# Two chained attention layers on one core: reciprocals and block transpositions by pairs of heads, low parts as steps of their own, and a newly drawn order of all steps

## What is computed

```python
# layer 0
h = jnp.concatenate([x, latents], axis=1)
q = (latents @ q_w + q_b).reshape(b, k_len, NH, DH)
kv = (h @ kv_w + kv_b).reshape(b, p + k_len, NH, DH, 2)
attn = jnp.einsum('bkhd,bnhd->bhkn', q, kmat) / DH
attn = softmax(where(full_mask, attn, -inf))
attn_out = jnp.einsum('bhkn,bnhd->bkhd', attn, v).reshape(b, k_len, H) @ out_w + out_b + residual
out = rmsnorm(attn_out, postnorm_w)
out = gelu(out @ mlp_w1 + mlp_b1) @ mlp_w2 + mlp_b2 + residual
# layer 1, on that result
xn = (input - mu) * rsqrt(var + EPS) * gamma + beta
att = softmax(einsum('nhqc,nhkc->nhqk', q * scale, k * scale))
y = einsum('nhqk,nhkc->nhqc', att, v)
out = input + einsum('co,nos->ncs', Wo, y) + bo
```

## Time and profile before

| | |
|---|---|
| median of 3 runs | 673.29 us (672.45 to 673.97) |
| the profiled execution, its own time | 670.9 us |
| its span, first to last instruction | 669.1 us |
| PE busy | 590.7 us, 88% |
| DVE busy | 575.9 us, 86% |
| ACT busy | 491.9 us, 74% |
| POOL busy | 402.8 us, 60% |
| mean granted TensorE clock | 0.962 |

### The profile page before, as it was taken

The page is one execution under the profiler, slowest core; times in us unless marked ns, Lnnn a source line. Parts: engine busy times, 40 slices in busy tenths (PEclk is TensorE's granted clock), DMA queues, the critical chain, the costliest instruction groups (busy, mean ns, idle before and its releaser), DMA issues.

```text
span 669.1 us, 21092 instructions
## 1 busy us (share of the span) xinstructions
PE 590.7 (88%) x8436; PEld 471.7 (70%) x8436; DVE 575.9 (86%) x1358; ACT 491.9 (74%) x1875; POOL 402.8 (60%) x392
## 2 busy tenths in 40 slices
PE   3597798799899989999899989999899989898985
PEld 3487776687688767776678667877678767676763
DVE  4685689699978999699987999799987999689993
ACT  1655777868787876878777876879778777867781
POOL 0520438477648857577548857578547857467672
PEclk9777997899999999999999999999999999898987
DMA  9700000011111111111111021111101121010110
GB/s 270 149 33 2 32 18 2 17 30 50 29 41 35 28 45 47 27 42 38 29 42 33 25 49 26 50 41 34 26 16 34 26 50 26 17 26 18 31 37 9
DMA packets 49826, 26.46 MB, mean 40 GB/s; under 512 B 37792, under 2 KB 48064, under 8 KB 49728
## 3 DMA queue, kind: packets, MB, share of 16 engines
q1 hardware_dynamic: 49728, 25.11, 14.6%
HBM read 22.99 MB, written 2.10 MB: 38 GB/s over the span
## 4 chain that ended last, share of the span: by engine, by line
PE 44%; DVE 40%; ACT 8%; DMA 3%; issue 2%; POOL 2%; SPq 1%
PE bank L561 42%; DVE nm L998 10%; DVE E1b L1007 8%; DVE nm L862 4%; DVE hm L882 4%; ACT E1b L1135 3%; DVE QS L991 2%; DMA E1b<-in_w 2%; ACT E L1065 2%; PE bank L681 2%; DVE ZS L1013 1%; ACT hm L1104 1%; DVE rs L1003 1%; DVE aos L808 1%; DVE xnb L983 1%
## 5 line engine op out<-in xcount | busy, mean ns | idle before, releaser
L1192 POOL TENSOR_TENSOR E1b<-E1b,rs 128x512 f32<-128x512 f32 x256 | 267.1, 1066 | 104.4 <-DVE rs L1003 100.4
L1135 ACT ACTIVATE E1b<-bank,nm 128x256 f32<-128x256 f32 x512 | 237.6, 499 | 72.9 <-DVE nm L998 72.6
L1007 DVE STREAM_TRANSPOSE E1b<-E1b 128x512 f32<-128x512 f32 x256 | 170.3, 688 | 2.7 <-POOL E1b L1192 1.9
L998 DVE TENSOR_REDUCE nm<-bank 128x2 f32<-128x512 f32 x256 | 165.4, 672 | 5.3 <-PE bank L561 4.7
L561 PE MATMUL bank<-E1b,CT 32*64 32x256 f32 x4096 | 124.2, 390 | 21.7 <-ACT E1b L1135 10.2
L561 PE MATMUL bank<-ctx,QS 64*128 64x256 f32 x1024 | 139.0, 400 | 3.2 <-ACT QS L1125 1.6
L561 PEld LDWEIGHTS bank<-E1b,CT 32*64 32x64 f32 x4096 | 98.3, 136 | 42.6 <-ACT E1b L1135 12.2
L1135 ACT ACTIVATION_READ_ACCUMULATOR E1b<-bank,nm 128x1 f32 x512 | 118.1, 231 | 0.0
L561 PEld LDWEIGHTS bank<-ctx,QS 64*128 64x128 f32 x1024 | 93.6, 190 | 28.6 <-issue 6.9
L1065 ACT ACTIVATE E<-bank,nm 128x128 f32<-128x128 f32 x256 | 90.4, 405 | 19.6 <-DVE nm L862 19.6
L1162 POOL TENSOR_TENSOR E<-E,rs 128x512 f32<-128x512 f32 x56 | 58.9, 1055 | 39.0 <-DVE rs L868 38.8
(11 more groups left out here) (103 smaller groups left out, 785.1 us busy)
## 6 DMA issues: line engine op xcount, KB each, us to landing
CT<-in_hT SPq DMA_DIRECT2D x256, 32.0 KB, 1.8
hraw<-in_hT SPq DMA_DIRECT2D x8, 512.0 KB, 3.2
ctx<-in_ctx SPq DMA_DIRECT2D x16, 256.0 KB, 3.9
xnat<-in_xn SPq DMA_DIRECT2D x8, 256.0 KB, 2.7
E1b<-in_w SPq DMA_DIRECT2D x2, 1024.0 KB, 11.7
out<-y SPq DMA_DIRECT2D x16, 128.0 KB, 1.8
E1b<-in_kvw SPq DMA_DIRECT2D x2, 256.0 KB, 4.4
mski<-in_msk SPq DMA_DIRECT2D x32, 1.0 KB
```

The lines of the kernel that those rows point to most:

```text
L998: e.tensor_reduce(nm1[:, u % 16, :], bank[place["S", u]][:, :].rearrange("p (i t) -> p i t", i=2), AX.X, ALU.max, negate=True).then_inc(dv ...
L1007: e.transpose(E1b[:, u % 16, :, :], E1b[:, u % 16, :, :]).then_inc(dve_steps, 1)
L1135: t = e.activation(E1b[:, r, i, :], bank[bk][:, i * 256:(i + 1) * 256], ACT.Exp, bias=nm1[:, r, i:i + 1], scale=1.0, accum_out=sum1[:, r, ...
L1192: e.tensor_tensor(E1b[:, u % 16, :, :], E1b[:, u % 16, :, :], rs1[:, u % 16, :].unsqueeze(2).to_broadcast([128, 2, 256]), ALU.mult).then_i ...
```

## The change

- `N` and `U` are steps of two units: one reciprocal of 128x4 and one transposition of 128x1024 where there were two of each. `N` waits for both exponentials, `U` for both rescalings.
- `hlo` is a step of its own that GpSimd or DVE may run; the mask row is a new step `mk`. `K`, `Q`, `V` wait for `hlo`, the scores `s` for `mk`. The next load `lh` is issued after both.
- The split of the attention output becomes `xo` (high part, ACT or DVE) and `xol` (low part, GpSimd or DVE).
- `SHIFT` may hold values for group 0 alone (names that end in 0), and the planner counts TensorE's steps 1.6 times in the first 60 us of its time (`COLD`). `SHIFT`, `LATE`, `PREP`, `COST`, `HEADAT` and `STAY` have new numbers, so the whole order is another.

```diff
-NP = ('POOL',)
+COLD = (60000, 1.6)
-PREP = 9
-LATE = (-4, -3, 2, 0, 0.5, 4, 3, 3)
-STAY = 1.5
+PREP = 10
+LATE = (-4, -3, -1, 0.5, -0.5, 4, 3, 4)
+STAY = 1
-HEADAT = -40
+HEADAT = -100
-    "hhi": (760, 840), "hlo": (1750, 1830), "wk": (1030, 1110), ...
+    "hhi": (760, 840), ("hlo", "DVE"): (1550, 1630), ("hlo", "POOL"): (2500, 2550), "mk": (210, 290), ...
...
+                    if e == "PE" and now < COLD[0]:
+                        hold, lasts = int(hold * COLD[1]), int(lasts * COLD[1])
...
-        add("hlo", g, on=A, at=at(), after=[("hhi", g), None if g else ("m0",)] + (
+        add("hlo", g, on=G + A, at=at(), after=[("hhi", g)])
+        add("mk", g, on=A, at=at(), after=[("lh", g) if g else ("m0",)] + (
             [("s", g - 2, c) for c in range(2)] if g >= 2 else []))
...
-        add("xo", g, on=A, at=at(), after=[("o1", g, c) for c in range(2)] + ([("O", g - 1)] if g else []))
+        add("xo", g, on=P + A, at=at(), after=[("o1", g, c) for c in range(2)] + ([("O", g - 1)] if g else []))
+        add("xol", g, on=G + A, at=at(), after=[("xo", g)])
...
-            add("N", u, on=A, at=u + LATE[3], after=[("E", u)])
-            add("Np", u, on=NP, at=u + LATE[4], after=[("N", u)])
-            add("U", u, on=A, at=u + LATE[5], after=[("Np", u)])
+            if h % 2:
+                add("N", u - 1, on=A, at=u + LATE[3], after=[("E", u - 1), ("E", u)])
+                for i in (u - 1, u):
+                    add("Np", i, on=G, at=i + LATE[4], after=[("N", u - 1)])
+                add("U", u - 1, on=A, at=u + LATE[5], after=[("Np", u - 1), ("Np", u)])
...
                     load_h(g)
+                    w.wait_ge(*done("mk", g - 1))
                     load_mask(g)
...
-                    e.reciprocal(rs1[:, u % 16, :], sum1[:, u % 16, :]).then_inc(dve_steps, 1)
+                    e.reciprocal(rs1[:, k:k + 2, :], sum1[:, k:k + 2, :]).then_inc(dve_steps, 1)
...
-                    e.transpose(E1b[:, u % 16, :, :], E1b[:, u % 16, :, :]).then_inc(dve_steps, 1)
+                    e.transpose(E1b[:, k:k + 2, :, :], E1b[:, k:k + 2, :, :]).then_inc(dve_steps, 1)
```

More of the change, by code:

```diff
@@ L48 @@
     "var": (130, 300), "q": (853, 1100), "S": (860, 1050), "Z": (3700, 3900), "Y": (1715, 1950),
[3 rows of a table removed]
[2 rows of a table added]
+    "hhi": (760, 840), ("hlo", "DVE"): (1550, 1630), ("hlo", "POOL"): (2500, 2550), "mk": (210, 290), "wk": (1030, 1110), "wq": (1030, 1110), "wv": (1030, 1110),
     ("Qe", "DVE"): (802, 890), "qs": (400, 500), "smax": (608, 692), "sn": (85, 169),
-    ("snp", "DVE"): (610, 694), "o1": (401, 480), "obtd": (3800, 3880), "w1": (1600, 1680),
[4 rows of a table removed]
+    ("snp", "DVE"): (850, 930), "o1": (401, 480), "obtd": (3800, 3880), "w1": (1600, 1680),
+    "w2": (1050, 1130), "Me": (601, 683), "WSe": (600, 680), "uue": (250, 330), "Mg": (400, 480), ("xo", "DVE"): (450, 530), ("xo", "ACT"): (500, 620), ("xol", "DVE"): (900, 980), ("xol", "POOL"): (1290, 1330),
[3 rows of a table added]
     "pw": (4330, 4400), ("snp", "POOL"): (999, 1045), "xop": (2950, 3000),
@@ L79, in add @@
         self.todo.append(step)
-        self.after[step], self.on[step], self.at[step] = [a for a in after if a], on, at + SHIFT.get(name, 0)
+        self.after[step], self.on[step], self.at[step] = [a for a in after if a], on, at + SHIFT.get(name, 0) + (
+            SHIFT.get(name + "0", 0) if key and key[0] == 0 else 0)
         self.banks[step], self.empties[step], self.kind[step] = banks, empties, kind
@@ L228, in plan @@
             p2, p1 = back(g, c, 2), back(g, c, 1)
-            add("s", g, c, on=V, at=at(1.0), after=[("Qe", g, 1), ("Ke", g, 0), ("Ke", g, 1), ("hlo", g)] + [
+            add("s", g, c, on=V, at=at(1.0), after=[("Qe", g, 1), ("Ke", g, 0), ("Ke", g, 1), ("mk", g)] + [
                 prev("t", p2, r) for r in range(4)],
@@ L627, in _ @@
                     pb = take("K", g, m)
-                    w.wait_ge(*last([("hlo", g), ("wk",)]))
+                    w.wait_ge(*done("hlo", g))
+                    w.wait_ge(*done("wk"))
                     for kt in range(2):
@@ L635, in _ @@
                     pb = take("Q", g)
-                    w.wait_ge(*last([("hlo", g), ("wq",)]))
+                    w.wait_ge(*done("hlo", g))
+                    w.wait_ge(*done("wq"))
                     for m in range(2):
@@ L645, in _ @@
                     pb = take("V", g, u)
-                    w.wait_ge(*last([("hlo", g), ("wv",)]))
+                    w.wait_ge(*done("hlo", g))
+                    w.wait_ge(*done("wv"))
                     for i in range(2):
@@ L657, in _ @@
                     w.wait_ge(*done("Qe", g, 1))
-                    w.wait_ge(*done("hlo", g))
+                    w.wait_ge(*done("mk", g))
                     if back(g, c, 2):
@@ L696, in _ @@
                     pb = take("O", g)
-                    w.wait_ge(*last([("xo", g), ("obtd",)]))
+                    w.wait_ge(*done("xol", g))
+                    w.wait_ge(*done("obtd"))
                     for u in range(2):
@@ L773, in _ @@
                     pb = take_all(*(("Z", n, r) for r in range(4)))
-                    w.wait_ge(*last([("U", 8 * n + h) for h in range(8)]))
+                    w.wait_ge(*last([("U", 8 * n + h) for h in range(0, 8, 2)]))
                     w.wait_ge(d_ct[n % 2], 128 * (n // 2 + 1))
@@ L924, in _ @@
                         w.wait_ge(*done("O", g - 1))
-                    split(aos[0][:, :, :, :], aos[1][:, :, :, :], AO[:, :, :, :]).then_inc(dve_steps, 1)
+                    e.tensor_copy(aos[0][:, :, :, :], AO[:, :, :, :]).then_inc(dve_steps, 1)
+                elif name == "xol":
+                    g, = key
+                    w.wait_ge(*done("xo", g))
+                    e.tensor_tensor(aos[1][:, :, :, :], AO[:, :, :, :], f(aos[0][:, :, :, :]),
+                                    ALU.subtract).then_inc(dve_steps, 1)
                 elif name == "yy":
@@ L1084, in _ @@
                                  scale=sm("par")[:, 0:1]).then_inc(act_steps, 1)
+                elif name == "xo":
+                    g, = key
+                    w.wait_ge(*last([("o1", g, c) for c in range(2)]))
+                    if g:
+                        w.wait_ge(*done("O", g - 1))
+                    e.copy(aos[0][:, :, :, :], AO[:, :, :, :]).then_inc(act_steps, 1)
                 elif name == "yn":
```

35 lines of the change are left out of this document (25 added, 10 removed), and 12 rows, old and new, of the table COST.

## The result

| | before | changed |
|---|---|---|
| median | 673.63 us (4 runs, 672.45 to 677.57) | 709.69 us (4 runs, 708.70 to 714.38; a fifth took 707.41) |
| the profiled execution | 670.9 us, span 669.1 | 714.38 us, span 712.6 |
| periods (32 units and a group) | 75.9 us | 82.5 to 83.9 us |
| first units' maxima on DVE | 98.16 us | 109.55 us |

What follows compares the result with a forecast made beforehand. It took a chain of waits through DVE (41.6 us), then TensorE (some 30 us), to bound each period. Six periods -11.4, start +3.0 and end -0.5 gave -8.9 us, so 664.4 us for the median, range 651 to 679.

Steps and rivals of the forecast that it cites:

- some +1.3, to 61.0: ACT's work in a period: steps given and taken add 1.3 us, to 61.0, leaving over 10 us of cover.
- TensorE's 71.3: TensorE's busy time in a period, 71.3 us, taken as unchanged and as the floor of a period.
- The start, +3.0: Start of the program: maxima wait behind group 1's mask row, 5.3 us later, 2.3 regained; +3.0, bounds -2 and +7.
- -1.9 us of DVE a period: DVE's work in each middle period: -6.4 + 4.5 = -1.9 us, to 68.0; bounds +0.5 and -3.9.
- I take the 1.9 in full: Each period shortens by all 1.9 us, though only some 40 of 76 us of the chain are DVE's.
- two entries that I called surely on the chain: `hlo` as the last link and the cast of the attention output, leaving DVE: 1.4 us of the 1.9.
- the relief becomes waiting: Rival: DVE's 1.9 us are saved beside TensorE's 30 us and the start is covered; 673 us, no change; chance 0.08.
- Rival 3: GpSimd becomes a link: `hlo` there delays rescalings by 2.6 us, +0.7 a period, 680.5 us; chance 0.20.
- Its first mark: Sign in the profile after: GpSimd's rescaling with more of the chain; no size given.
- Its second: Sign in the profile after: DVE waiting for GpSimd's rescaling at L1029; no size given.
- The end, -0.5: Units after 552 us: -1.0 from less DVE work on the chain, +0.5 from the last pair's waits; -0.5 us.

Runs made afterwards that it cites:

- a_both: Changed kernel with each group's four gelus together on ScalarE and the second mask row ahead of the next h's high part: 671.08 us, 1.0006.
- a_gelu: Changed kernel with one edit on ScalarE's queue, the four gelus of a group together with no exponential between: 682.34 us, 1.015.
- a_hlo: Changed kernel with the low part of h on DVE in all groups, right behind the high part: 731.09 us, 1.0905.
- b_low: Kernel before, own order, with mask row and low parts as own steps and, from group 3 on, h's low part on GpSimd: 680.60 us, 1.0128.
- b_pair: Kernel before, own order, with only the paired reciprocals and transpositions, each where the second head's step stood: 687.70 us, 1.021.

## Why the prediction was wrong

**The step that failed** is "ACT gives four `QD` and takes two `te`, four `ze`, a `qe` and the cast: some +1.3, to 61.0 ... Both keep over 10 us of cover." The steps were counted, but not the loads that an order of steps brings about: four more in a period, 5.1 us. ACT went to 66.7. And the cover was taken as an average over a period, where the loads fell in one place, between gelus whose banks TensorE waits for. The order of ACT's instructions would have told it: exponential between gelus is visible without running anything, and the 1.28 us stand in the profile before. The Trainium skill (ScalarE: Activation LUTs, on what the load costs and in its rules for authors) says to do all of one set before switching, and gives 1283 ns for the load and another 1380 for a drain. The first number is that of every load here; of the second nothing shows, as the gelu begins at 200.36 behind a load of 1.28 that began at 199.07.

**TensorE's 71.3** rose to 74.0 by the clock, which the prediction held constant. It goes with the pause: with the gelus together (a_both), TensorE was busy for 6.57 of the 8.41 us in the gap, kept a clock of 1.00, and had 71.2.

**The start, +3.0**, was the right mechanism with sizes too small. I had the mask's load landing at 26.0, with a bound of 28.5, and the maxima at 29.7; it was used at 31.48, above the bound, and they came at 36.10. The prediction had the queue free for these loads at 18.6 and the landing 4.1 us behind; the queue came to h of group 1 only at 21.55, and the mask row began 9.9 us behind that. With the same order at the start, a_gelu had 19.18 for the queue and 27.16 for the mask row, with the maxima at 31.77, and a_hlo 19.95 and 27.1. So the mask row moves by 4 us between executions, and the profiled one, 4.7 us above the median, is the late one of three. Of the first units' delay, 3.0 expected, 11.4 (here) and 7.2 (a_gelu) were measured. Taken away alone it is worth 3 to 8 us, with the gelus together 10 to 11 (by ratios and by medians).

**-1.9 us of DVE a period** was right as work (67.15 to 68.24 against 68.0 said; the pair's transposition 1.224 against 1.24 in the text's marks), and was not a gain. "I take the 1.9 in full" failed too. Of the two entries that I called surely on the chain, `hlo` moved in the old order cost time (b_low): on GpSimd it is 2.37 us of chain in place of 1.12 on DVE; the cast was not tried alone. The pairs put into the old order (b_pair) cost time as well, where the reciprocal and transposition wait for the second head. The repaired kernel is the rival "the relief becomes waiting" (671 us; it said 673, with a chance of 0.08). For the kernel as it is no rival held: none had ACT in it.

**Rival 3** named the wrong side with the right sign. Its first mark, more of the chain on GpSimd, is absent (1%). Its second is there: DVE waits 11.1 us for GpSimd at L1029, where it was 1.9 before. But a_both has the same 11.1 us and no loss, and a_hlo refutes the rival for the new order; b_low shows something like it, +9 us, in the old one.

**The end, -0.5**: measured +0.5 in 117.6 us.

The accounts: loads in the periods and the start together explain the 36 us, by a_both. That the changes of the work themselves balance at zero is measured as a sum, too. How this zero is made up is known for the pairs alone (-17 in the new order); what single heads lose in it against the kernel before, 17 us, belongs to the order, the split steps and the moved ones together, and was not taken apart further, except that its chain crosses ACT for 8.4 us a period.

## What to carry to other kernels

When a change redraws an order, read each engine's new sequence for what the order itself brings: switches of ScalarE's tables, loads in front of a queue, and which instruction empties the banks that TensorE takes next. Here the switches of one order cost more than any single edit of the work did; a planner whose costs leave them out has no reason to avoid them. A pair, or a step moved to an idle engine, has no price of its own: pairs cost 16 us in one order and saved 17 in another.

## What the runs showed of the hardware

- A change of table is 1.283 us and follows its neighbours without a gap. 22 of them taken out of the changed kernel gave 25 to 27 us; 20 put into the kernel before cost 36, with what they and the exponentials beside them held up.
- TensorE's granted clock was 0.50 for 4 us and 0.74 for 4 more behind 13.6 us in which it was busy for 7.7 with the last 5.5 idle, and stayed at 1.00 behind 8.4 us with 6.6 busy (a_both). The pause was thus paid for twice.
- A DVE subtraction of two operands took 2.71 us beside a GpSimd one, and 0.69 alone. The Trainium skill (SBUF — State Buffer, on the shared port pair) says that the second one waits for the whole of the first. The trace agrees: GpSimd's ran from 5.05 to 7.55, and DVE's, begun at 5.38, ended at 8.09, 0.54 behind it.
- A mask load of four times 1 KB behind large ones was used at 31.48, 27.16 and 27.1 us in three executions with the same order up to there (the changed kernel, a_gelu, a_hlo).
